# Group attention in a seven-phase fp32 kernel: one phase's order of work rewritten as a pipeline over iterations

## The reference

```
q = x @ Wq + bq                    # 32 heads of 16 features
k = ctx @ Wk + bk; v = ctx @ Wv + bv   # 8 heads of 16, each for 4 query heads
attn = softmax(q k^T / 4 + mask)   # 128 x 128 for each head
out = (attn v) @ Wo + bo + x
y = (out - mean(out)) * rsqrt(var(out) + 1e-6) * gamma + beta
```

## Time and profile before

| | |
|---|---|
| median of 3 runs | 3706.64 us (3705.56 to 3712.22) |
| the profiled execution: its time | 3707.4 us |
| the profiled execution: its span | 3705.6 us |
| mean granted TensorE clock | 0.949 |
| PE / DVE / ACT / GpSimd busy | 88% / 48% / 30% / 23% |
| group phase, first DMA issue to end of the last DVE instruction | 1251.5 to 1747.8 us, 496.3 us |

### The profile page before, as it was taken

The page is one execution under the profiler, slowest core; times in us unless marked ns, Lnnn a source line. Parts: engine busy times, 40 slices in busy tenths (PEclk is TensorE's granted clock), DMA queues, the critical chain, the costliest instruction groups (busy, mean ns, idle before and its releaser), DMA issues. The chain is left out here.

```text
span 3705.6 us, 52772 instructions
## 1 busy us (share of the span) xinstructions
PE 3278.6 (88%) x19344; PEld 2160.1 (58%) x19344; DVE 1776.9 (48%) x2532; ACT 1121.7 (30%) x4036; POOL 857.2 (23%) x574
## 2 busy tenths in 40 slices
PE   7999789979999877775799999999689999899999
PEld 5565455646676554543666666666445555466665
DVE  4555355430000256665478888888635545410000
ACT  2434233321121244543223323332223333311111
POOL 2333133310000000010355555556300000000000
PEclk9999899989999888887899999999899999999999
DMA  3110131110000131011101111111013101010010
GB/s 146 47 40 28 46 139 48 49 52 23 14 20 17 40 137 48 24 43 43 41 28 40 47 35 35 45 46 33 18 66 125 38 30 37 24 34 26 25 34 11
DMA packets 103587, 168.87 MB, mean 46 GB/s; under 512 B 16432, under 2 KB 53936, under 8 KB 100016
## 3 DMA queue, kind: packets, MB, share of 16 engines
q1 hardware_dynamic: 98576, 123.27, 10.4%
q10 hardware_dynamic: 4896, 44.04, 2.9%
HBM read 133.72 MB, written 33.55 MB: 45 GB/s over the span
## 5 line engine op out<-in xcount | busy, mean ns | idle before, releaser
L1704 POOL TENSOR_TENSOR rec_S<-rec_S,rec_r_t 128x1024 f32<-128x1024 f32 x128 | 309.8, 2420 | 315.1 <-DVE rec_S L1984 315.1
L1984 DVE TENSOR_TENSOR_SCAN rec_S<-rec_decay,rec_S 128x1024 f32<-128x1024 f32 x128 | 321.6, 2513 | 22.7 <-ACT rec_S L1774 19.4
L1390 PE MATMUL mlp_bank<-mlp_src_t,region_a 128*128 128x256 f32 x1024 | 224.3, 381 | 1.7 <-ACT mlp_src_t L1315 1.7
L1390 PE MATMUL pmlp_bank<-pmlp_src_t,region_a 128*128 128x256 f32 x1024 | 224.4, 381 | 1.3 <-ACT pmlp_src_t L1315 1.3
L547 ACT ACTIVATE group_scores<-group_scores,group_negmax 128x128 f32<-128x128 f32 x512 | 197.4, 391 | 79.5 <-DVE group_negmax L737 79.3
L1402 PE MATMUL mlp_bank<-region_a,mlp_h_t 128*128 128x512 f32 x512 | 221.1, 592 | 0.0
L1402 PE MATMUL pmlp_bank<-region_a,pmlp_h_t 128*128 128x512 f32 x512 | 221.1, 592 | 0.0
L1390 PEld LDWEIGHTS mlp_bank<-mlp_src_t,region_a 128*128 128x128 f32 x1024 | 195.9, 191 | 32.1 <-issue 5.5
L1390 PEld LDWEIGHTS pmlp_bank<-pmlp_src_t,region_a 128*128 128x128 f32 x1024 | 195.9, 191 | 31.7 <-issue 5.0
L1360 DVE TENSOR_TENSOR mlp_y<-mlp_bank,mlp_xres 128x512 f32<-128x512 f32 x16 | 11.1, 692 | 380.3 <-PE mlp_bank L1402 380.3
L1360 DVE TENSOR_TENSOR pmlp_y<-pmlp_bank,pmlp_xres 128x512 f32<-128x512 f32 x16 | 11.1, 692 | 369.4 <-PE pmlp_bank L1402 369.4
(11 more groups left out here) (329 smaller groups left out, 6604.5 us busy)
## 6 DMA issues: line engine op xcount, KB each, us to landing
rec_vb<-v_by_head SPq DMA_DIRECT2D x32, 512.0 KB, 4.2
region_a<-in_C_w ACTq DMA_DIRECT2D x2, 4096.0 KB, 19.8
region_a<-in_G_w ACTq DMA_DIRECT2D x2, 4096.0 KB, 19.7
self_x<-in_x SPq DMA_DIRECT2D x16, 256.0 KB, 3.2
self_xres<-in_x SPq DMA_DIRECT2D x16, 256.0 KB, 2.6
rows_A<-self_xres SPq DMA_DIRECT2D x16, 256.0 KB, 2.0
cross_x<-rows_A SPq DMA_DIRECT2D x16, 256.0 KB, 3.2
cross_ctx_t<-in_ctx_t SPq DMA_DIRECT2D x16, 256.0 KB, 3.1
```

The lines of the kernel that those rows point to most:

```text
L1390: product = nc.tensor.matmul(ph.bank(item)[:, i * TT:(i + 1) * TT], W1[:, c, f:f + 128], src_t[:, c, :, :], start=c == 0, stop=c == C - 1)
L1704: nc.gpsimd.tensor_tensor(S[u % 4][:, :, :], S[u % 4][:, :, :], bcast(r_t[:, s.k, UNITS[u][0], :], [128, JH, T], 1), ALU.mult)\
L1984: nc.vector.tensor_tensor_scan(St[:, :, :].rearrange(flat), decay[m][:, :, :].rearrange(flat), St[:, :, :].rearrange(flat), 0.0, ALU.mult, ...
```

## The change

`group` leaves `attention_phase` for a function of its own, `group_phase`, with the same arithmetic, tiles and buffers. What differs:

1. **Order over iterations.** The scores, mask and maxima of a unit stand two units ahead of its transposes: body `it` does units 2 and 3 of `it` and units 0 and 1 of `it + 1`, one inside each unit's transposes. The exponentials stand one unit ahead.
2. **Rows two ahead.** `transpose_rows` of `it + 2` instead of `it + 1`; `keys` and `queries` of `it + 1` as before.
3. **Output by sequence.** `output`, statistics, power and norm run for each sequence separately.
4. **Gamma and beta on GpSimd.** DVE's `output_norm` is one instruction (subtract, multiply by rstd, into `o`); `scale_output` on GpSimd does the two others. All 16 copies are on DVE.
5. Bank uses follow the new order; `values(0)` of bank A and `values(1)` of bank B remain. SP loads each mask half as soon as its units are read, and a residual when the norm has read the old one.

```diff
-            attention_phase(nc, GROUP, const, rC, rD, ctx_t, a["mask_group"], a["bv_group"], D_w, D_load, E_load)
+            group_phase(nc, GROUP, const, rC, rD, ctx_t, a["mask_group"], a["bv_group"], D_w, D_load, E_load)
...
+        body_uses += [("A", ("v", 0), 0), ("A", ("q", 0), 1), ("A", ("q", 1), 1), ("A", ("k", 0), 1),
+                      ("A", ("k", 1), 1), ("A", ("out", 1), -1), ("A", ("out", 0), 0),
+                      ("B", ("v", 1), 0), ("B", ("pv", 0), 0), ("B", ("pv", 1), 0)]
...
+            def scale_output(it, k):
+                pool.wait_ge(normed, it * 2 + k + 1)
+                nc.gpsimd.tensor_tensor(o[:, k, :], o[:, k, :], row("g_gamma"), ALU.mult).then_inc(scaled, 1)
+                pool.wait_ge(scaled, it * 2 + k + 1)
+                nc.gpsimd.tensor_tensor(o[:, k, :], o[:, k, :], row("g_beta"), ALU.add).then_inc(y_done, 1)
...
+            def body(it):
+                if not is_first(it):
+                    scale_output(it - 1, 0)
+                spread_inverse(it, 0)
+                residual_bias(it, 0)
+                if not is_first(it):
+                    norm_scale(it - 1, 1)
+                spread_inverse(it, 1)
+                if not is_first(it):
+                    scale_output(it - 1, 1)
+                residual_bias(it, 1)
+                norm_scale(it, 0)
...
+            def body(it):
+                later = has_later(it, 1)
+                exponentials(it, 1, 0)
+                exponentials(it, 1, 1)
+                if later:
+                    query_features(it + 1, 0)
+                exponentials(it, 2, 0)
+                exponentials(it, 2, 1)
+                if later:
+                    query_features(it + 1, 1)
+                exponentials(it, 3, 0)
+                exponentials(it, 3, 1)
+                if later:
+                    exponentials(it + 1, 0, 0)
+                if has_later(it, 2):
+                    rows_features(it + 2)
+                if later:
+                    exponentials(it + 1, 0, 1)
```

More of the change, by code:

```diff
@@ L122, in use @@
             uses[b] += 1
-        for b, item in before:
-            use(b, item, 0)
+        for b, item, it in before:
+            use(b, item, it)
         for it in range(NIT):
@@ L346, in attention_phase @@
         pj = Banks("pj", sem, {b: ps(f"pj{b}", [128, BANK]) for b in "ABPQ"},
-                   before=[("P", ("x", 0)), ("Q", ("x", 1))] +
-                          [("A", (w, n)) for w, items in (("q", 2), ("k", k_items)) for n in range(items)],
+                   before=[("P", ("x", 0), 0), ("Q", ("x", 1), 0)] +
+                          [("A", (w, n), 0) for w, items in (("q", 2), ("k", k_items)) for n in range(items)],
                    body=body_uses, after=[("A", ("out", 1))])
```

494 lines of the change are left out of this document (added), and 3 rows, old and new, of the table through_identity.

## The result

The changed kernel takes **3614.61 us** (median of 4 runs, 3611.02 to 3616.86); the kernel before took 3707.12 in the same comparison (4 runs, 3705.56 to 3712.22). The ratio is 0.9747, interval 0.973 to 0.9764: faster by 92.5 us. The forecast was 3616, within 3598 to 3658. The profiled execution took 3611.02 us, with a span of 3609.2 and a mean granted clock of 0.964 (before 0.949).

A forecast was written before the change was run, and what follows sets the result against it. No engine was full; DVE and PE alternated, waiting on each other. Start to 1283.9, iteration 0 about 41, six periods of 47.0, last iteration and tail to 1655: 93 us less, 2 given back, 3707.4 - 91 = 3616 us, range 3598 to 3658.

The forecast's parts named there:

- a unit is a chain across both engines: Group phase: work passes between DVE and PE within each unit, so neither engine's sum (PE 40.7, DVE 37.6 us) is reached.
- The walk: Steady iteration followed by measured durations at full clock: units of 10.9, 8.9, 14.6 and 11.2 us, together 45.6.
- The engines' sums: Work per iteration after the change: PE 40.7 us, DVE 37.6, GpSimd 10.4, ACT below 28.6.
- The clock: Steady iterations: 1.4 us for a clock below 1.00 and loose handoffs, from the walked 45.6 to a period of 47.0.
- Iteration 0: First iteration of the group phase, without a predecessor's output: about 41 us, to 1325.
- The sum: Group phase from start to tail: last DVE instruction at 1655 instead of 1747.8, 93 us less.
- edges not walked: Allowance over the whole group phase: 2 us given back, making the saving 91 instead of 93 us.
- Unit 2: The longest unit, 14.6 us: second key block frees bank A, only then half a of outputs, 1.9, and scores, 1.15.
- Unit 3: Unit of 11.2 us: half a of outputs 1.9, then product, row transpose and scores 1.95, then mask to second maximum 5.35.
- Longer chains: Rival, 20%: one more wait of 1.4 us in each unit, period about 53, 3658 us.
- The low clock: Rival, 4%, on the slower side: PE falls to the low clock and stays there.
- GpSimd slows the norm: Rival, 10%, within the forecast: sequence 1's norm on DVE beside GpSimd's `spread_inverse`, at most 8 us, 3624 us.

The follow-up runs named there:

- e3: The changed kernel with the next iteration's scores put ahead of the first half of the outputs in units 2 and 3; 3601.72 us.
- e7: e4 with the 13 loads of the next phase's weights issued by SP instead of ACT; 3591.29 us.
- e1: The kernel before, old order kept, with only gamma and beta moved to GpSimd; 3683.28 us.
- e9: The kernel before with two of four chunks left out of every query matmul of the group phase; 3683.28 us.
- e4: e3 with DVE's norm of sequence 1 behind the mask instead of before it; 3595.65 us.
- e8: e7 with unit 0's scores ahead of the values of sequence 1 on PE and its mask ahead of the third copy on DVE; 3585.64 us.
- e10: e8 with two of four chunks left out of every query matmul of the group phase; 3569.97 us.
- e2: The changed kernel (new order) with gamma and beta back on DVE; 3633.84 us.
- e6: The changed kernel with one of two chunks left out of every half of the outputs; 3605.97 us.
- e5: The changed kernel with two of four chunks left out of every query matmul of the group phase; 3605.98 us.

## Why the prediction held, and where it did not

**The mechanism.** That "a unit is a chain across both engines" is shown three ways: PE's work cut by 3.1 us gives 0.68, the exchanges of e3 on PE, without any less work, give 2.57, and 2.8 us of DVE work cost 2.36 where the norms stand. The walk gave 45.6 for a steady period of 45.67.

**The engines' sums.** PE was put at 40.7 and is busy 40.1; DVE at 37.6, busy 38.15, of which 0.5 is the longer norm of sequence 1; GpSimd at 10.4, busy 10.8; ACT below 28.6, 27.6. PE's sum holds a small misreading: the half of the queries, 1.93, was taken from the start of its weight load at 1488.17, while its matmuls began at 1488.28, 1.82 before the product. Of the 40.7, 15.0 are 16 pairs of a product (0.36 to the next transpose, 1490.10 to 1490.46) and a transpose (0.58 to the next product, 1490.46 to 1491.04). The kernel after shows 0.36 (1317.56 to 1317.92) and 0.59 (1307.74 to 1308.33) for them, at clock 1.00.

**The clock.** The forecast's period of 47.0 is the walk's 45.6 and 1.4 us for a clock below 1.00 and for loose handoffs. The 1.4 was an estimate that no run shows: from iteration 3 on the clock was 1.00 and the period 45.67. In iterations 1 and 2 it was 0.96, and iteration 2 took 46.06, 0.4 more than a steady one. Over iterations 1 to 6 the mean period is (1608.54 - 1333.16) / 6 = 45.9, against 47.0. This term was mis-sized by 1.1, six times: 6.6 us too much.

**Iteration 0** was put at 41 and took 1327.89 - 1283.16 = 44.7. PE in the kernel after:

```profile
1311.72 0.66 PE L1725 MATMUL group_pjB<-group_probs_t,group_v 128*32 128x128 f32 x8 [2.97 <-DVE group_probs_t L1538]
...
1314.07 3.56 PE L1689 MATMUL group_pjA<-region_b,group_o_t 128*128 128x512 f32 x4
...
1318.50 1.15 PE L1702 MATMUL group_sc<-group_k_pair,group_q_t 32*128 32x256 f32 x16
```

PE waited 2.97 us for a copy; behind that wait the granted clock was 0.50 and 0.52 (1311.7 to 1314.1 and from there to 1317.6), the outputs took 3.56 instead of 1.98, and the mask after the scores had waited 4.71. The step "about 41" was worked out at clock 1.0 throughout. With the scores ahead of these outputs (e3) the same mask waited 1.36.

**The sum.** First copy 1283.2 (put at 1283.9); start of iteration 1 1327.9 (1325); of the last 1603.4 (1607); end of the phase 1652.9 (1655). So the start took 0.7 less, iteration 0 3.7 more, the six in the middle 6.5 less and the last with the tail 1.4 more (49.5 for 48): 2.1 less in all, by errors of opposite sign. The 2 us "for edges not walked" weren't needed, and 1.5 of the difference between the spans lies behind the phase. The profiled time is thus 5.4 below the 3616.4 that the sum gives; the median of the runs, which is 3.6 above the profiled one, is 1.4 below the forecast. That it is so close is luck: single terms were off by up to 6.6 us.

**Unit 2** was named the longest for the right reason. **Unit 3** was walked with a wrong member: "half a of outputs 1.9" was taken to set its scores, and it does so only in a tie with the copy and product (halving it gave 0.12). The length came out right because both ended at the same moment.

**Gamma and beta** "2.8 us an iteration at most": 2.36 measured in the new order, 2.7 in the old. A pass takes longer on GpSimd (1.27 for 0.69), and still both comparisons show a gain, 19 and 22 us, since GpSimd was mostly idle (busy 5.3 us of an iteration in before, 10.8 of 45.67 in after) and DVE on the chain. The result of the pass is only stored, so its length stands beside the chain, and of the time taken off DVE 2.36 of 2.8 us count.

**The rivals.** Longer chains did not come (28.9 us of waits for copies are left of 67.3). The low clock came for single stretches in iterations 0 to 2 (0.50 at 1311.7, 1363.2 and 1421.2) and did not stay: from iteration 3 on it was 1.00. That GpSimd slows the norm came as described, for sequence 1 alone (1.04; sequence 0 kept 0.54), and cost nothing in this kernel. The one that began later became longer: GpSimd's pass began at 1502.75 and ended at 1503.80, the norm began at 1503.05 and ended at 1504.09, 0.29 after it. That is less than the 0.54 that the norm takes alone, so the rows don't show that all of it waited for the pass to end, and what held it up isn't shown. In the recurrence phase of the kernel before, a norm stands ahead of a GpSimd pass:

```profile
1902.12 0.52 DVE L1937 TENSOR_SCALAR rec_x<-rec_x,rec_stats,rec_rstd 128x512 f32<-128x512 f32 x1
...
1902.28 2.59 POOL L1704 TENSOR_TENSOR rec_S<-rec_S,rec_r_t 128x1024 f32<-128x1024 f32 x1 [3.49 <-DVE rec_S L1984]
```

The norm began first and took 0.52, and the GpSimd pass took 2.59, where the same pass at 1895.93, with no norm beside it, took 2.36.

**The signs to look for.** Period, clock, unit 2, GpSimd and the norm are as named; DVE's wait for PE before its copies is 16.4 + 5.5 = 21.9 us, under the 25 given (read the other way, as PE's wait for the copies, it is 28.9 and over). "ACT's wait for maxima no longer ahead of any transpose" holds only roughly: ACT still waited 51.2 us for maxima, but steady iterations have only short waits of transposes for exponentials, such as 0.17 us at 1511.18, and 0.5 at most in the weight loads.

## What to carry to other kernels

When no engine is full, write the order of the two engines that alternate as one chain and walk it by measured durations; the sum of the walk told this period to 0.1 us (its units to 0.4), where the engines' busy sums (40 and 38) lay 6 to 8 us below it. Then look at the longest wait of the bounding engine and ask what stands on the other engine ahead of the instruction it waits for: if it's work whose result nobody needs soon, exchange the two, which here gave 2.6 us an iteration for no change in work. Each such exchange pays until the thing overtaken becomes the next one waited for, so look at the following gap as well as at the one that was shortened.

## What the runs showed of the hardware

- **The issue of DMAs held an engine.** In after, thirteen loads took ACT's queue 12 us, 1.93, 2.32 and 2.27 for the last three, and the exponentials behind them stood for 10.08. With SP issuing them (e7) the seven periods were 1.7 shorter.
- **The granted clock followed the order of the work.** In iteration 0 PE waited 2.97 us, and the outputs behind it ran at a granted clock of 0.52, 3.56 for 1.98. In before it was 0.50 over the 6 us from 1469.00, with DVE busy 5.43 of them and PE 2.75. In the old order the mean of an iteration stayed at 0.85 to 0.91 where GpSimd had taken work over (e1) and at 0.83 to 0.87 where PE's own was cut (e9). In the new order it was 0.96 and then, from iteration 3 on, 1.00 in after, and 1.00 from iteration 1 on in e3, e4, e7, e8 and e10, the last with 3 us less work on PE. It stood lower in most iterations of e2 (0.93 to 0.97, one at 1.00), in some of e6 (0.92 to 1.00) and in the last two of e5 (0.96), with more work on DVE or less on PE; why there and not in e10 isn't shown. For the same matmuls PE's busy time is 45.3 in an iteration of e1 and 40.1 in one of after.
- **A norm of 128x512 that reads and writes SBUF takes 0.54 us, begun beside a GpSimd pass 1.04** (1503.05 in after; 0.52 where it began first, at 1902.12 in before); copies and masks that read PSUM kept their 0.68 and 2.3 (the mask at 1480.96 beside the pass at 1481.82, the copy at 1478.07 beside the one at 1478.23).
